# A power instead of a sum in GpSimd's pause between row transfers

## What is computed

```
x = x + L0_attn(layernorm(x))        # 16 query heads of 8, 4 key/value heads, causal
x = x + L0_ffn(layernorm(x))         # top-1 of 8 experts, 128 -> 2*512 -> 128, silu(a)*g
x = x + L1_attn(layernorm(x))        # latent keys/values (32), rotary, 16 heads of 8, causal
x = x + L1_ffn(layernorm(x))         # top-2 of 8 experts, 128 -> 512 -> 128, relu, biases
```

## Time and profile before

| | |
|---|---|
| time, median of 3 runs | 976.34 us (975.29 to 977.66) |
| span of the profiled execution | 1059.9 us |
| busy: PE, PEld | 902.2 us (85%), 600.8 us (57%) |
| busy: DVE, ACT, POOL | 667.9 us (63%), 610.0 us (58%), 534.5 us (50%) |
| the pause, L1023 | 62 instructions, 210 ns each, 13.0 us |
| the indirect transfers, L1090, L1098, L1108 | 96, 78 and 32 |

### The profile page before, as it was taken

The page is one execution under the profiler, slowest core; times in us unless marked ns, Lnnn a source line. Parts: engine busy times, 40 slices in busy tenths (PEclk is TensorE's granted clock), DMA queues, the critical chain, the costliest instruction groups (busy, mean ns, idle before and its releaser), DMA issues.

```text
span 1059.9 us, 25406 instructions
## 1 busy us (share of the span) xinstructions
PE 902.2 (85%) x8968; PEld 600.8 (57%) x8968; DVE 667.9 (63%) x1379; ACT 610.0 (58%) x1173; POOL 534.5 (50%) x809
## 2 busy tenths in 40 slices
PE   4699999879998999889998999978998776399791
PEld 2344554436995445349974454534447766388781
DVE  1889897857457888855669987997861351011116
ACT  3168897825445786734346867856784343155541
POOL 3144454562015776752137855676865633744442
PEclk9999999879999899789999989998988888699996
DMA  5635523353755253519844273345023445357577
GB/s 145 138 85 161 152 70 88 83 162 108 216 170 125 92 144 86 128 43 302 234 133 81 84 160 93 95 116 149 28 61 90 143 133 152 99 164 217 164 211 226
DMA packets 137317, 141.20 MB, mean 133 GB/s; under 512 B 35564, under 2 KB 113452, under 8 KB 137100
## 3 DMA queue, kind: packets, MB, share of 16 engines
q1 hardware_dynamic: 130604, 126.04, 43.7%
q0 software_dynamic: 6592, 13.55, 4.1%
HBM read 98.73 MB, written 44.36 MB: 135 GB/s over the span
## 4 chain that ended last, share of the span: by engine, by line
PE 30%; DVE 6%; another core or an unknown queue 5%; issue 5%; SPq 4%; ACT 3%; DMA 2%; POOL 0%; DVEq 0%; ACTq 0%; POOLq 0%
PE psum L1317 8%; PE psum L1327 7%; PE psum L1248 4%; DVE neg_max L1510 2%; PE psum L1204 2%; PE psum L1230 2%; SPq L963 1%; ACT scratch L1439 1%; SPq L962 1%; PE psum L1210 1%; PE psum L1274 1%; SPq L933 1%; SPq L916 1%; PE psum L1283 1%
## 5 line engine op out<-in xcount | busy, mean ns | idle before, releaser
L1510 DVE TENSOR_REDUCE neg_max<-psum 128x2 f32<-128x768 f32 (+3 forms) x352 | 380.7, 1120 | 73.2 <-PE psum L1210 52.2
L1439 ACT ACTIVATE scratch<-psum 128x1024 f32<-128x1024 f32 x320 | 316.7, 1024 | 97.2 <-PE psum L1230 84.3
L1079 POOL TENSOR_SCALAR_AFFINE_SELECT scratch<-scratch 128x512 f32<-128x512 f32 x256 | 159.0, 642 | 150.8 <-ACT scratch L1439 149.6
L1317 PE MATMUL psum<-rows_t,w_now 128*128 128x128 f32 x1360 | 177.6, 284 | 5.3 <-issue 2.2
L1248 PE MATMUL psum<-scratch,values 128*32 128x512 f32 (+3 forms) x2048 | 173.4, 460 | 1.3 <-POOL scratch L1079 0.3
L1317 PEld LDWEIGHTS psum<-rows_t,w_now 128*128 128x128 f32 x1360 | 165.6, 198 | 13.8 <-issue 8.8
L1327 PE MATMUL psum<-w,hidden_t 128*128 x992 | 140.7, 292 | 36.4 <-ACT hidden_t L1476 15.5
L1204 PE MATMUL psum<-k_stack,q_stack 52*128 52x128 bf16 (+3 forms) x1024 | 136.2, 326 | 25.7 <-DVE neg_max L1510 10.2
L1476 ACT ACTIVATE hidden_t<-psum,w_now 128x128 f32<-128x128 f32 x312 | 88.7, 372 | 115.0 <-remote 39.6
L1327 PEld LDWEIGHTS psum<-w,hidden_t 128*128 128x128 f32 x992 | 128.0, 204 | 43.4 <-issue 43.2
L1230 PE MATMUL psum<-q_stack,k_stack 55*128 55x512 bf16 (+3 forms) x1024 | 124.9, 316 | 14.5 <-DVE neg_max L1510 5.6
(11 more groups left out here) (141 smaller groups left out, 1027.5 us busy)
## 6 DMA issues: line engine op xcount, KB each, us to landing
w_now<-in_w SPq DMA_DIRECT2D x78, 322.0 KB
w_now<-in_w SPq DMA_DIRECT2D x46, 512.0 KB
q_stack<-q_parts SPq DMA_DIRECT2D x64, 192.0 KB
q_parts<-q_parts SPq DMA_DIRECT2D x16, 384.0 KB, 3.2
k_stack<-k_parts SPq DMA_DIRECT2D x32, 192.0 KB
q_parts<-q_parts SPq DMA_DIRECT2D x16, 256.0 KB, 3.0
w<-in_w SPq DMA_DIRECT2D x16, 256.0 KB, 4.5
scratch<-returned SPq DMA_DIRECT2D x16, 256.0 KB, 3.6
```

Source lines behind the costliest of these rows:

```text
L1079: pool.affine_select(out=diag, in_=diag, compare_op=ALU.is_ge, fill=0.0, base=0, pattern=[[0, 4], [1, P]], channel_multiplier=-1).then_inc ...
L1317: ins = pe.matmul(bank[v.bank][:, c * P:(c + 1) * P], w1_now[layer][w.slot][:, n * FFN + c * P:n * FFN + (c + 1) * P], rows)
L1439: act.activation(expd[s.slot], psum[:, u.bank:u.bank + 2, :], ACT.Exp, scale=SCALE).then_inc(read[u.bank], 1)
L1510: return dve.tensor_reduce(out=out, in_=in_, axis=AX, op=op, negate=negate)
```

## The change

The pause's operation becomes a power: `consts[:, C_EPS] ** consts[:, C_HALF]` in place of their sum. Operands, size, output, waits and place in the order stay.

```diff
@@ -1020,7 +1020,7 @@
 
                 if pauses[0]:
                     pool.wait_ge(paused, pauses[0])
-                pool.tensor_tensor(r_small[:, 2, 0:QT], consts[:, C_EPS:C_EPS + QT], consts[:, C_HALF:C_HALF + QT], ALU.add).then_inc(paused, 1)
+                pool.tensor_tensor(r_small[:, 2, 0:QT], consts[:, C_EPS:C_EPS + QT], consts[:, C_HALF:C_HALF + QT], ALU.pow).then_inc(paused, 1)
                 pauses[0] += 1
 
             for s in plan.order("pool"):
```

## The result

The changed kernel takes 990.04 us in the median of four runs (987.19 to 993.40) against 975.92 us (975.29 to 977.66) for the kernel before: ratio 1.0148, 95% interval 1.0116 to 1.0180. The forecast was 979.5 us, its range ended at 987 us.

What follows compares the result with a forecast made beforehand. The prediction saw the chain of waits spread over TensorE, with GpSimd's transfers mattering only where others wait for them. Its terms, 1.15 + 1.0 + 0 + 1.0 = 3.2 us on 976.34 us, gave 979.5 us; range 964 to 987 us.

## What to carry to other kernels

Before pricing a longer instruction in an in-order queue, list for every instruction behind it who reads its result and what stands in that reader's own queue behind the wait; the loss here came through a mark of 0.17 us on VectorE, and through masks for which TensorE waited 3.88 us and then ran at the lower clock. When a stall leaves TensorE idle, add the slow matmuls after it to the price: here 2.2 us on 3.9. And when a profile is 8% longer than the times beside it, don't choose a cause before the same kernel has been timed and recorded on one chip: the same change lost 14 us on some chips, and its parts gained 6 to 35 us on others. No version here was measured to beat both; the power before every fifth transfer costs nothing that can be told from noise where there are no stalls (976.8 beside 977.6 and 978.0 beside 974.7 us), and whether it removes them where there are wasn't seen.

## What the runs showed of the hardware

The kernel before has two times, 975 to 978 us on chips 2 and 5 and 1060 to 1063 us on chips 3, 0 and 14, and most of the difference lies where GpSimd issues row transfers 1.3 us apart. Beside a free chip's trace of about the same time (the sum before every transfer, chip 2), the profile before takes 10 us more from the first scatter to the first gather (118.1 against 108.2 us) and 51 us more from the first scatter of the tail to the last send (253.7 against 202.8). Another 19 us (459.7 against 440.7) lie between, where the runs of transfers are mostly split by masks. Only part of it goes with the pauses there: 461.9 us with sums in 5 to 8 and 451.2 with the power, both on chip 0. What takes the rest isn't known. In a stall TensorE, VectorE and ScalarE are busy for less, and SyncE's own issues slow down: four loads take SyncE 4.18 us to issue on chip 5 and 8.62 us in a stall on chip 14.

```profile
842.78 4.18 SPq L963 DMA_DIRECT2D rows_in<-sorted_in  x4
```

```profile
898.42 8.62 SPq L963 DMA_DIRECT2D rows_in<-sorted_in  x4
```

A gap of 1.3 us between pairs (from 909.16 to 910.43 us with the power in the sends, chip 14) removes the stall in that place, one of 0.4 us doesn't (135.3 us for the 63 sends against 135.9 us with no pause). Whether the gap or the average rate decides, and what it is that the engines share there, stays open.

A power on GpSimd costs 571 ns over 128x1 and 1041 ns over 128x4 in the median, a sum over 128x4 207 to 208 ns.
